# A two-layer graph network on one core: mended table rows for tied nodes, and edge slots that begin at any edge, fetched by SyncE at register addresses

## The chip, the core and the metric

The kernel runs on one core of one Trainium2 chip. The metric is the time on the device in microseconds (us), the median over several runs. The engines are TensorE (PE; its weight loads are PEld), VectorE (DVE), ScalarE (ACT), GpSimd (POOL) and SyncE (SP). They work in parallel, each through its own list of instructions in order, and wait for each other by semaphores. DMAs are issued from the lists of SP and POOL (a few from ACT) and move data beside them.

## The reference, cut to what matters

There are 3125 nodes of 256 features and 50000 edges sorted by their destination. Two layers follow each other:

```python
h = relu(layernorm(x))                              # layer 0
m = relu(h @ W_pool.T + b_pool)[src] * weight       # one row per edge
neigh = segment_max(m, dst); neigh = where(deg > 0, neigh, 0)
x = x + h @ W_self.T + b_self + neigh @ W_neigh.T + b_neigh

h = relu(layernorm(x))                              # layer 1
e = edge_emb[edge_type]                             # 16 types
messages = (h[src] + e) @ msg_W + msg_b
ew = 1 + edge_scale * tanh(gelu(concat(h[src], h[dst], e, task) @ att_W1 + att_b1) @ att_W2 + att_b2)
agg = segment_sum(scaled(messages) * ew, dst) / max(segment_sum(ew, dst), 1)
x = x + layernorm(h + mlp(concat(h, scaled(agg)))) * ln_g + ln_b
```

## The kernel before, in words

The nodes lie in 28 windows (NT) of 112 nodes (WIN), in 7 groups (NG) of 4 windows (GN). The program has five parts, called stages here.

**Stage 1** makes the rows that are gathered in layer 0 (`hp_d`, in HBM).

**The chain** (lines 424 to 1137) computes the segment maximum. Each of the 128 partitions owns a run of 391 edges (CH). In step j POOL gathers one row of 256 for each partition (line 683, a ring of 6 buffers of 4 steps, so POOL may be 24 steps ahead), ACT multiplies by the weight (716), and DVE keeps a running maximum that restarts where a new destination begins (924). SP stores the states in pieces of 8 steps (line 635, piece number q, 49 of them) to the table `hist_d`; the buffers of the states are a ring of 2, so step 8(q+2) waits until piece q has landed. The row of the table at a node's last edge is its maximum. Beside the chain DVE, PE and ACT do small jobs at step numbers written out by hand (`J_...`): the number of slots of each window, indices, products of weights. SP has loads between its stores, among them three at q = 24 and four at q = 28.

A node can span the border of two partitions. For these ties a scan over the partitions after the last step (1133) gives `carry`, the maximum that comes in from the partitions before. PE's step `choose(i)` (1365) places the carry rows for each window by a product with the one-hot `tied`, and DVE's `merge(i)` (1600) takes the maximum of them and the gathered rows.

**Edge slots.** The last-but-one stage works on slots of 128 edges that belong to one window. Before, a slot begins at a multiple of 32 edges (BLK): source, destination and type of the edges are written as blocks of 32 to `blocks_d`, the wanted blocks are gathered by POOL (1337, 14 gathers), written to `rec_d`, read back one group of 4 slots per partition (1295), and DVE turns them into rows (`slot_fields`, 1642); PE transposes them (`turn_fields`, 1425, 12 transposes) and DVE copies them out (`take_fields`, 1657). The number of slots is fixed at build time for the worst case: 425 slots in 107 groups, the last group with one slot.

**The node stage** (first half of the block from line 1226) loops over i = 0 to 6. POOL gathers the table rows of a group of windows (420, four gathers), `merge` mends them, PE transposes them (`turn_n`, 1376) and multiplies by W_neigh (`neigh`, 1385), DVE adds to x and takes the statistics (`rows_x`), POOL takes the inverse root (`root`, 1322), DVE makes the shifts (1623), ACT makes h (`rows_h`, 1521), PE transposes h (`turn_h`, 1396) and makes the tables of layer 1 (`messages`, 1408; `keys_q`, 1421 for i = 1 to 3, the other four at the end). PE's order is written out by hand: turn_n(i+1), turn_h(i), neigh(i+1), keys_q(i-1), three of four messages, choose(i+2), the last message. POOL's order is node_rows(i+2), root(i), record gathers. `keep_warm` are matmuls whose result nobody reads.

**The edge stage** does for each group of 4 slots: POOL gathers 128 rows of `pm_d` per slot (1354, a ring of 6 groups), PE makes z of each slot from the window's keys (1477, three products whose right side is at a register address) and the gathered rows (1479), ACT takes gelu (1565), DVE the dot product with W2 (1737), ACT the weights (1579 to 1586), PE sums by destination (1501) and DVE adds to `acc` at a register address (1724). The window numbers come to PE and DVE by a load of four registers per group (line 396). At every seventh group from group 6 on, 14 times, PE and ACT also do a pair of windows of another product (1490).

**The last stage** (from 1743) is the update of the nodes and the layernorm.

Of the kernel before, what the change touches and what calls it, by code (L numbers as in the profile page):

```python
# [6 lines left out]
def gnn_two_layers(nc, A, out):  # L7
# [15 lines left out]
    GN = 4  # L23
# [5 lines left out]
    BLK = 32  # L29
# [3 lines left out]
    NB = ER * ROW // BLK  # L33
    SG = 4
    RB = P // BLK
    SLOTS = (E + NT * (BLK - 1 + P - 1)) // P
# [3 lines left out]
    assert NGR <= P  # L40
    RC = -(-SLOTS * RB // P)
# [13 lines left out]
    hist_d = nc.dram_tensor("hist_d", [P * CH + 1, D], fp32, kind="Internal").ap()  # L55
    link_d = nc.dram_tensor("link_d", [P], fp32, kind="Internal").ap()
    blocks_d = nc.dram_tensor("blocks_d", [NB + 1, FLD * BLK], fp32, kind="Internal").ap()
    want_d = nc.dram_tensor("want_d", [RC * P], i32, kind="Internal").ap()
    rec_d = nc.dram_tensor("rec_d", [RC * P, FLD * BLK], fp32, kind="Internal").ap()
# [21 lines left out]
    with top:  # L81
# [38 lines left out]
        want = sbt("want", [P, RC], i32)  # L120
# [285 lines left out]
        keep = acc[0:WIN, after_nt + D:after_nt + D + NT]  # L406
# [9 lines left out]

        def node_rows(eng, i, to):
            for k in range(GN):
                t = i * GN + k
                eng.indirect_dma_start(to[:, k * D:(k + 1) * D], None, hist_d[:, :],  # L420
                                       bass.IndirectOffsetOnAxis(ap=end_i[:, t:t + 1], axis=0)).then_inc(ngot[i % 4], 16)

        b2 = ExitStack()
        with b2:
# [32 lines left out]
            end_0 = s("end_0", [WIN, NT], fp32)  # L457
            tied_b = s("tied_b", [P, WIN], fp32)
            tied_w = s("tied_w", [P, NT], fp32)
            tied = up[:, 2560:2560 + NT * WIN]  # L460
# [7 lines left out]
            blk = acc[0:ER, 8 * ROW:(8 + FLD) * ROW]  # L468
            junk = acc[:, 13 * ROW:14 * ROW]
            blk4 = blk.rearrange("p (b f e) -> p b f e", f=FLD, e=BLK)  # L470
            padb = s("padb", [1, FLD * BLK], fp32)
            cnt = s("cnt", [ER, NT + 1], fp32)
            j_i = s("j_i", [NGR, SG], i32)
            r_i = s("r_i", [NGR, SG * RB], i32)
            jf = s("jf", [NGR, SG], fp32)
            rf = s("rf", [NGR, SG * RB], fp32)
            s_f = s("s_f", [NGR, NT + 1], fp32)
            s_i = s("s_i", [NGR, NT + 1], i32)
            fb_i = s("fb_i", [NGR, NT + 1], i32)
            fb = s("fb", [NGR, NT + 1], fp32)  # L480
# [8 lines left out]
            wantf = s("wantf", [NGR, SG * RB], fp32)  # L489
            want_i = s("want_i", [NGR, SG * RB], i32)  # L490
            want_pad = s("want_pad", [1, RC * P - SLOTS * RB], i32)
# [9 lines left out]
            ngot = [sem2(f"ngot{r}") for r in range(4)]  # L501
            prep = sem2("prep")
# [27 lines left out]
            blk_ready = sem2("blk_ready")  # L530
            blk_out = sem2("blk_out")
# [1473 lines left out]
```

## Time and profile before

| What | Value |
|---|---|
| Time, median of 3 runs | 1336.85 us (1335.12 to 1338.69) |
| Profiled execution, its own time as the trace has it: the span | 1333.1 us |
| Mean granted TensorE clock | 0.80 of full speed |
| Busy shares | PE 71%, DVE 70%, POOL 65%, ACT 46% |
| DMA | 266.84 MB, mean 200 GB/s |
| Instructions | 18946 |

The trace is of one execution. Its span runs from the first to the last instruction; the timed runs lie some 2 to 6 us above it. In the rows further down, the number behind "idle" or in square brackets is the time that the engine had stood idle just before, with what ended it. In the timeline the columns are start, duration, engine, line, operation, tiles and count; consecutive instructions of one kind are merged into one row whose duration runs over all of them.

### The profile page before, as it was taken

The page shows a single profiled execution, that of the slowest core. Times are in us where ns is not written, and L with a number is a line of the kernel's source. Part 1 is how long each engine was busy: PE and PEld are TensorE (multiplying, and loading weights), DVE is VectorE, ACT ScalarE, POOL GpSimd, SP SyncE. Part 2 cuts the span into 40 slices and gives each one's busy share as a digit, 9 for nine tenths or more (in the row PEclk, how much of TensorE's full clock was granted, in tenths as well). Part 3 has the DMA queues.
Part 4 walks back from the last instruction along what each step waited for, and adds up shares of the span by engine and source line. Part 5 has one row for each costly group of instructions (what it writes and reads, how often), then busy time and mean ns, then how long its engine had stood idle before and what let it go on. Part 6 is the DMA issues. An engine that isn't in the chain of part 4 may idle for free. (4 is left out here: it accounts for less than half of the span.)

```text
span 1333.1 us, 18946 instructions
## 1 busy us (share of the span) xinstructions
PE 946.2 (71%) x5112; PEld 734.5 (55%) x5112; DVE 927.7 (70%) x2671; ACT 615.5 (46%) x1494; POOL 867.5 (65%) x884
## 2 busy tenths in 40 slices
PE   7405455555123511189997999999999999999984
PEld 6402233333012510177775777777777777777773
DVE  6466475666466554346756888888888888888758
ACT  6334333433333433323324666665656566666554
POOL 0377777777777777665237777777777777777112
PEclk9755555555555555599998999999999999999988
DMA  5667667557676665534657778778777877777322
GB/s 154 135 206 261 208 213 206 198 201 234 211 278 213 210 199 197 206 87 121 159 155 226 229 231 235 231 232 237 232 231 231 239 234 228 233 234 230 94 68 83
DMA packets 105353, 266.84 MB, mean 200 GB/s; under 512 B 25101, under 2 KB 45940, under 8 KB 99108
## 3 DMA queue, kind: packets, MB, share of 16 engines
q0 software_dynamic: 54560, 166.61, 42.7%
q1 hardware_dynamic: 48900, 97.26, 22.8%
q10 hardware_dynamic: 1792, 1.75, 0.5%
q8 instruction: 47, 0.77, 0.2%
q14 instruction: 54, 0.44, 0.1%
HBM read 195.59 MB, written 68.81 MB: 198 GB/s over the span
## 5 line engine op out<-in xcount | busy, mean ns | idle before, releaser
L683 POOL DMA_INDIRECT gath<-hp_d,chain_src x391 | 386.3, 988 | 169.3 <-issue 157.7
L1354 POOL DMA_INDIRECT gbuf<-pm_d,srcs x357 | 343.8, 963 | 114.7 <-issue 104.9
L924 DVE SCALAR_TENSOR_TENSOR hist<-hist,smask,gath 128x256 f32<-128x256 f32 x390 | 189.2, 485 | 207.4 <-ACT gath L716 199.6
L716 ACT ACTIVATE gath<-gath,chain_w 128x256 f32<-128x256 f32 x391 | 167.4, 496 | 335.3 <-DMA gath<-hp_d,chain_src 335.2
L1724 DVE TENSOR_TENSOR acc<-ps,acc 112x272 f32 x425 | 186.8, 440 | 70.2 <-DVE acc L1724 62.9
L1477 PE MATMUL ps<-qw,halves 128*128 x1275 | 209.9, 274 | 8.1 <-DVE halves L1709 8.1
L1479 PE MATMUL ps<-gbuf,ident 128*128 128x256 f32 x714 | 214.2, 382 | 0.0
L1565 ACT ACTIVATE gbuf<-ps 128x512 f32<-128x512 f32 x180 | 107.4, 597 | 163.8 <-PE ps L1479 163.8
L1501 PE MATMUL ps<-gbuf,placed 128*112 128x272 f32 x714 | 179.6, 393 | 0.9 <-issue 0.6
L839 PE MATMUL ps<-win_hot,node_hot 128*112 128x28 bf16 x391 | 43.6, 253 | 187.6 <-DVE win_hot L1023 187.6
L1477 PEld LDWEIGHTS ps<-qw,halves 128*128 128x128 bf16 x1275 | 125.0, 98 | 80.0 <-issue 11.2
L839 PEld LDWEIGHTS ps<-win_hot,node_hot 128*112 128x112 bf16 x391 | 39.9, 207 | 193.9 <-DVE win_hot L1023 192.6
L1501 PEld LDWEIGHTS ps<-gbuf,placed 128*112 128x112 f32 x714 | 125.6, 177 | 36.6 <-DVE acc L1724 2.8
L1737 DVE CUSTOM_DVE_ANT_0 gbuf<-gbuf,w2b 128x256 f32<-128x256 f32 x357 | 134.1, 427 | 10.2 <-ACT gbuf L1565 10.2
L1586 ACT ACTIVATE placed<-placed,logit 128x112 f32<-128x112 f32 x425 | 130.2, 377 | 3.5
L1479 PEld LDWEIGHTS ps<-gbuf,ident 128*128 128x128 f32 x714 | 108.5, 192 | 4.1
L765 PE MATMUL ps<-wsT,hT_s 128*112 128x256 f32 x112 | 57.2, 666 | 58.5 <-ACT hT_s L727 48.5
L1354 POOL DMA_INDIRECT attw<-pm_d,srcs x68 | 66.5, 978 | 21.6 <-issue 19.8
L765 PEld LDWEIGHTS ps<-wsT,hT_s 128*112 128x112 f32 x112 | 30.0, 298 | 79.8 <-issue 63.2
L1728 DVE TENSOR_TENSOR placed<-ps,edgef 128x448 f32<-128x448 f32 x107 | 65.8, 615 | 0.0
L1821 POOL TENSOR_TENSOR rs_c<-ve_c,power 112x4 f32<-112x4 f32 x7 | 12.5, 1788 | 75.2 <-DVE ve_c L1951 75.2
L1021 DVE TENSOR_TENSOR node_hot<-ps,low 128x896 bf16<-128x896 f32 (+1 forms) x49 | 52.9, 1081 | 0.0
(290 smaller groups left out, 1429.5 us busy)
## 6 DMA issues: line engine op xcount, KB each, us to landing
hist_d<-hist SPq DMA_DIRECT2D x48, 1024.0 KB, 4.5
gath<-hp_d,chain_src POOLq DMA_INDIRECT x391, 2.8
wn<-node_row_d SPq DMA_DIRECT2D x27, 224.0 KB
key<-node_row_d SPq DMA_DIRECT2D x26, 224.0 KB, 3.6
gbuf<-pm_d,srcs POOLq DMA_INDIRECT x357, 4.0
pm_d<-gbuf SPq DMA_DIRECT2D x6, 896.0 KB, 5.0
hb_d<-gbuf SPq DMA_DIRECT2D x7, 448.0 KB, 3.5
qw<-hb_d SPq DMA_DIRECT2D x7, 448.0 KB, 8.0
```

The source lines that it names most:

```text
L683: eng.indirect_dma_start(row_at(j), None, hp_d[:, :], bass.IndirectOffsetOnAxis(ap=chain_src[:, j:j + 1], axis=0)).then_inc(got[q % RINGG] ...
L716: eng.activation(row_at(j), row_at(j), ACT.Copy, scale=chain_w[:, j:j + 1]).then_inc(gw_ready, 1)
L765: ins = eng.matmul(bank(6, 2)[0:WIN, k * D:(k + 1) * D], hT[i % 2][:, (k * 2 + hf) * WIN:(k * 2 + hf + 1) * WIN], wsT[:, hf * D:(hf + 1) * ...
L924: eng.scalar_tensor_tensor(out=state_at(j), in0=state_at(j - 1) if j else first_state[:, :], scalar=smask[:, j:j + 1], in1=row_at(j), op0= ...
L1354: eng.indirect_dma_start(gath3(g % RING)[:, k, 0:2 * D], None, pm_d[:, :], bass.IndirectOffsetOnAxis(ap=srcs[:, g * SG + k:g * SG + k + 1] ...
L1477: eng.matmul(to, hot[g % 2][:, k * P:(k + 1) * P], qw[:, bass.ds(w[k] * (3 * D) + part * D, D)], start=part == 0, stop=False)
L1479: ins = eng.matmul(to, ident[:, :], gath3(r)[:, k, 0:D], start=False, stop=True)
L1501: eng.matmul(bank(4 + k)[0:WIN, 0:AW], place[q % 3][:, k * WIN:(k + 1) * WIN], gath3(q)[:, k, D:SW], start=True, stop=True).then_inc(sums_ ...
L1565: eng.activation(gath3(r)[:, 2 * half:2 * half + 2, 0:D], bank(2 * (g % 2) + half).rearrange("p (k d) -> p k d", k=2), ACT.Gelu)\
L1586: ins = eng.activation(at, at, ACT.Copy, scale=logit[q][:, k:k + 1])
L1724: eng.tensor_tensor(to, bank(4 + k)[0:WIN, 0:AW], to, ALU.add).then_inc(summed, 1)
L1737: ins = eng.tensor_tensor_reduce(zk, zk, w2b[:, :], 1.0, 0.0, ALU.mult, ALU.add, logit[r % 3][:, k:k + 1])
```

## The change

**Slots begin at any edge.** The blocks of 32 go. Source, destination and type are stored as three long rows (`fields_d`), and a slot is described by its first edge. The worst case falls to 418 slots in 105 groups, the last with two slots. In place of POOL's 14 block gathers, of `rec_d` and of its reading back, SP fetches each slot by a DMA of its own (3 runs of 512 bytes to one partition) whose address is in a register: 5 groups, that is 5 loads of four registers and 20 DMAs, after each of its stores from q = 24 to 44. `slot_fields` moves to chain step 376, `turn_fields` to PE's list ahead of the last matmuls of the chain, `take_fields` behind chain step 386; the row stores (`node_row_d`, `type_row_d`) move behind SP's last store of the chain.

**Tied nodes.** Only group 0 is still mended by `choose` and `merge`. For the other groups the 128 partitions' mended rows are computed once (one more POOL gather of the rows at the partitions' first ends, and one DVE maximum), stored by SP behind the table, and the row indices of tied nodes point there. POOL's gathers of group 1 now wait for that store.

```diff
-    SLOTS = (E + NT * (BLK - 1 + P - 1)) // P
+    SLOTS = (E + NT * (P - 1)) // P
...
-    hist_d = nc.dram_tensor("hist_d", [P * CH + 1, D], fp32, kind="Internal").ap()
+    hist_d = nc.dram_tensor("hist_d", [P * CH + 1 + P, D], fp32, kind="Internal").ap()
...
+            Q_SLOT, QG = 24, 5
+            J_ROWS = 376
+            J_COLS = J_ROWS + 4
...
+                def fetch_slots(n):
+                    if n == 0:
+                        eng.wait_ge(want_in, 32)
+                        eng.wait_ge(fld_out, 16)
+                    for g in range(n * QG, min(NGR, (n + 1) * QG)):
+                        regs = [eng.alloc_register(name=f"slot{g}_{k}") for k in range(SG)]
+                        eng.load(regs, starts[0:1, g * SG:(g + 1) * SG])
+                        for k in range(SG):
+                            e0 = eng.snap(regs[k], donate=True, min_val=0, max_val=E)
+                            eng.dma_start(flds3[g:g + 1, :, k * P:(k + 1) * P],
+                                          fields_d[:, bass.ds(e0, P)].rearrange("(a f) e -> a f e", a=1)).then_inc(slot_in[k], 16)
...
+                    if q >= Q_SLOT:
+                        fetch_slots(q - Q_SLOT)
+                eng.wait_ge(rows_ready, 2)
+                for d, t in ((node_row_d, row_n), (type_row_d, row_t)):
+                    for g0, g1 in ((0, EVEN), (EVEN, NGR)):
+                        eng.dma_start(d.rearrange("(g e) -> g e", g=NGR)[g0:g1, :], t[g0:g1, :]).then_inc(rows_out, 16)
...
                 node_rows(eng, 0, first_rows(0))
+                eng.indirect_dma_start(mend, None, hist_d[0:P * CH + 1, :],
+                                       bass.IndirectOffsetOnAxis(ap=first_end[:, 0:1], axis=0)).then_inc(mend_in, 16)
...
+                turn_fields()
                 eng.wait_ge(stepped, CH - 5)
                 for _ in range(14):
                     eng.matmul(bank(2)[:, 0:P], ident[:, :], ident[:, :], start=True, stop=True)
                 eng.wait_ge(stepped, CH)
+                eng.wait_ge(cols_taken, FLD)
...
+                    if j == J_ROWS:
+                        slot_fields()
+                    if j == J_COLS + 6:
+                        take_fields()
...
-                    t = at(j, J_LAST, 1, NT)
+                    t = at(j, J_LAST, 1, GN)
...
             def _(eng):
+                eng.wait_ge(mended, 1)
+                eng.dma_start(hist_d[P * CH + 1:P * CH + 1 + P, :], mend).then_inc(mend_out, 16)
                 eng.wait_ge(ngot[1], 16 * GN)
...
-                node_rows(eng, 1, first_rows(1))
                 eng.memset(power[:, :], -0.5).then_inc(power_set, 1)
                 eng.wait_ge(power_set, 1)
+                eng.wait_ge(mend_out, 16)
+                node_rows(eng, 1, first_rows(1))
...
                 def turn_n(i):
-                    eng.wait_ge(merged, i + 1)
-                    if i >= 1:
+                    if i == 0:
+                        eng.wait_ge(merged, 1)
+                    else:
+                        eng.wait_ge(ngot[i % 4], (i // 4 + 1) * (16 * GN))
                         eng.wait_ge(n_put, i)
...
-                choose(0)
+                choose()
                 keep_warm(12)
                 turn_n(0)
                 neigh(0)
-                choose(1)
-                keep_warm(8)
+                keep_warm(16)
                 for i in range(NG):
                     if i + 1 < NG:
                         turn_n(i + 1)
-                    if i == COL_AT:
-                        turn_fields()
                     turn_h(i)
                     if i + 1 < NG:
                         neigh(i + 1)
                     if 1 <= i <= QE:
                         keys_q(i - 1)
-                    messages(i, range(3))
-                    if i + 2 < NG:
-                        choose(i + 2)
-                    messages(i, range(3, GN))
+                    messages(i, range(GN))
...
+                def mend_rows():
+                    eng.wait_ge(mend_in, 16)
+                    eng.tensor_tensor(mend, mend, carry, ALU.max).then_inc(mended, 1)
...
-                merge(0)
+                merge()
+                mend_rows()
                 rows_x(0)
                 shifts(0)
-                merge(1)
```

Some small DVE jobs of the chain also change: 24 of 28 products for `tied` go, the slot arithmetic loses its block steps, and `tie` and `ends` get a few operations that count the first end of each partition and point tied nodes at their mended rows.

## Rows read from the trace of the kernel before

**Rows 1.** Busy time by stage, and of two short stretches, all engines
```profile
core 0: us, PE busy (x) PEld busy (x) DVE busy (x) ACT busy (x) POOL busy (x), PEclk, DMA share, GB/s
562.00:712.40 150.40, 132.70 (x690) 107.91 (x689) 89.47 (x169) 42.99 (x64) 71.65 (x65) 0.99 0.52 138
712.40:1250.00 537.60, 536.75 (x3064) 421.32 (x3064) 458.31 (x1576) 325.30 (x868) 395.78 (x412) 1.00 0.77 228
...
713.20:715.00 1.80, 1.75 (x7) 1.22 (x8) 1.17 (x3) 0.00 (x0) 1.45 (x2) 0.50 0.78 223
...
717.00:719.00 2.00, 2.00 (x15) 1.51 (x14) 0.88 (x5) 1.00 (x2) 1.70 (x2) 1.00 0.96 306
```
**Rows 2.** Line 683: ns min/median/max, first and last start
```profile
L683 POOL DMA_INDIRECT gath<-hp_d,chain_src x391: 942/946/2027, 52.4 to 556.7; - x196
```
**Rows 3.** Timeline, DVE in two groups of the edge stage, and its last sum
```profile
1228.25 0.61 DVE L1728 TENSOR_TENSOR placed<-ps,edgef 128x448 f32<-128x448 f32 x1
...
1233.23 0.62 DVE L1728 TENSOR_TENSOR placed<-ps,edgef 128x448 f32<-128x448 f32 x1
...
1259.18 0.44 DVE L1724 TENSOR_TENSOR acc<-ps,acc 112x272 f32 x1 [0.21 <-DVE acc L1724]
```
**Rows 4.** Timeline, POOL end of the chain, start of the mending
```profile
551.47 0.95 POOL L683 DMA_INDIRECT gath<-hp_d,chain_src  x1 [0.30 <-issue]
552.02 1.01 DVE L924 SCALAR_TENSOR_TENSOR hist<-hist,smask,gath 128x256 f32<-128x256 f32 x2
...
558.39 3.61 DVE L924 SCALAR_TENSOR_TENSOR hist<-hist,smask,gath 128x256 f32<-128x256 f32 x7 [5.36 <-ACT gath L716]
...
564.27 0.94 POOL L420 DMA_INDIRECT up<-hist_d,acc  x1 [6.68 <-DMA hist_d<-hist]
...
570.62 1.66 DVE L1600 SCALAR_TENSOR_TENSOR up<-ps,acc,up 112x256 f32<-112x256 f32 x4 [3.19 <-DMA up<-hist_d,acc]
...
581.45 1.05 POOL L1322 TENSOR_TENSOR acc<-acc,power 112x4 f32<-112x4 f32 x1 [2.62 <-DVE acc L1618]
...
585.15 0.93 PE L1396 MATMUL ps<-ident,gbuf 112*128 112x112 f32 x8
```
**Rows 5.** SP stores of line 635: ns min/median/max, and landings
```profile
L635 SPq DMA_DIRECT2D hist_d<-hist x51: 319/320/348, 74.9 to 562.0; - x51
...
DMA to landing us min/median/max: 2.0/4.4/8.3
```
**Rows 6.** take_fields and turn_fields, groups by line: busy, mean ns
```profile
L1662 DVE COPY edgef<-ps 128x428 f32<-128x428 f32 x2 | 1.1, 594 | 0.0
L1662 DVE CAST srcs<-ps 128x428 int32<-128x428 f32 x1 | 0.6, 594 | 0.0
...
L1431 PE MATMUL ps<-ident,qw 107*128 107x107 f32 x12 | 1.3, 255 | 0.0
```
**Rows 7.** Timeline, PE in the node stage
```profile
612.93 1.89 PE L1365 MATMUL ps<-acc,up 128*112 128x256 f32 x8
...
616.64 0.78 PEld L1376 LDWEIGHTS ps<-ident,gbuf 112*128 112x128 f32 x8 [0.51 <-DVE gbuf L1600]
...
634.52 0.78 PEld L1376 LDWEIGHTS ps<-ident,gbuf 112*128 112x128 f32 x8 [0.51 <-DVE gbuf L1600]
```
**Rows 8.** Timeline, PE at the start of the edge stage
```profile
713.25 0.82 PE L1477 MATMUL ps<-qw,halves 128*128 x3 [8.15 <-DVE halves L1709]
```
**Rows 9.** Register loads and address arithmetic of PE: ns min/median/max
```profile
L396 PEldq TENSOR_LOAD <-wins x107: 327/331/522, 712.0 to 1249.5; - x107
...
L1477 PEldq FUSED_REGOPS  x1275: 46/46/46, 713.1 to 1250.3; - x183
```
**Rows 10.** SP: small direct DMAs, and four loads at q = 28
```profile
L622 SPq DMA_DIRECT2D acc<-in_dst_dram x2: 268/272/275, 57.0 to 57.3; - x2
...
359.03 0.38 SPq L604 DMA_DIRECT2D acc<-in_L_gnn_ma_W_dram  x1
...
362.46 0.68 SPq L604 DMA_DIRECT2D acc<-in_L_gnn_ua_W_dram  x1
```

More of the change, by code:

```diff
@@ L39, in gnn_two_layers @@
     SLOTS = NGR * SG
-    assert NGR <= P
-    RC = -(-SLOTS * RB // P)
+    assert NGR <= P and E + P <= ER * ROW
     NPAD = 4000.0
@@ L536, in gnn_two_layers @@
             want_in = sem2("want_in")
-            recs_in = sem2("recs_in")
-            recs_out = sem2("recs_out")
-            nat_in = sem2("nat_in")
+            slot_in = [sem2(f"slot_in{r}") for r in range(4)]
+            shifted = sem2("shifted")
             rows_ready = sem2("rows_ready")
@@ L834, in type_messages, with turn_fields @@
                     ins.then_inc(tps, 1)
+                def turn_fields():
+                    eng.wait_ge(flds_ready, 1)
+                    for f, b in enumerate((6, 7, 4)):
+                        for k in range(SG):
+                            ins = eng.transpose(bank(b)[:, k * NGR:(k + 1) * NGR],
+                                                flds[:, f * GW + k * P:f * GW + (k + 1) * P], ident[0:NGR, 0:NGR])
+                        ins.then_inc(cols_ready, 1)
                 def count_ends(q):
@@ L1067, in tie @@
                     eng.tensor_scalar(tied_b[:, :], iof[:, 0:WIN], low[:, first], None, ALU.is_equal)
+                    eng.wait_ge(io_set2, 2)
+                    eng.tensor_copy(edge[:, 11:12], run_i[:, :])
+                    eng.tensor_scalar(off[:, :], own[:, :], own[:, first], 0.0, ALU.is_equal, ALU.add, accum_out=edge[:, 12:13])
                     after(eng.tensor_scalar(tied_w[:, :], iof[:, 0:NT], edge[:, 9:10], edge[:, 8:9], ALU.is_equal, ALU.mult))
+                    eng.tensor_scalar(tied_n[:, :], tied_w[:, :], edge[:, 11:12], None, ALU.mult)
+                    after(eng.scalar_tensor_tensor(out=edge[:, 13:14], in0=edge[:, 11:12], scalar=float(CH), in1=edge[:, 12:13],
+                                                   op0=ALU.mult, op1=ALU.add))
+                    eng.tensor_scalar(first_end[:, :], edge[:, 13:14], float(-(CH + 1)), None, ALU.add)
                 def ends(part):
@@ L1086, in ends @@
                                                        op0=ALU.add, op1=ALU.add))
+                        late = slice(GN, NT)
+                        after(eng.scalar_tensor_tensor(out=end_t[:, late], in0=bank(3)[0:WIN, late], scalar=float(P * CH),
+                                                       in1=end_f[:, late], op0=ALU.add, op1=ALU.subtract))
+                        after(eng.tensor_tensor(end_t[:, late], end_t[:, late], end_0[:, late], ALU.mult))
+                        after(eng.tensor_tensor(end_f[:, late], end_f[:, late], end_t[:, late], ALU.add))
                         eng.tensor_copy(end_i, end_f[:, :]).then_inc(ends_out, 1)
@@ L1178, in gnn_two_layers @@
             chosen = sem("chosen")
+            mended = sem("mended")
+            mend_out = sem("mend_out")
             merged = sem("merged")
@@ L1691, in _ @@
                         shifts(i + 1)
-                    if i + 2 < NG:
-                        merge(i + 2)
                     take(i, 3)
```

214 lines of the change are left out of this document (72 added, 142 removed).

## The prediction

> **What bounds the kernel now.** I read the busy time by stage first. The edge stage takes 537.6 us, and PE is busy for 536.8 of it at full clock; the node stage takes 150.4, with PE busy for 132.7, also at full clock [rows 1]. So both go at PE's pace, and there a PE instruction or a slot less is time. The chain is different: POOL issues 391 gathers from 52.4 to 556.7, one every 504.3 / 390 = 1.293 us [rows 2], and everything else in that stage only has to keep up, SP included. A piece of 8 steps lasts 10.34 us. The parts that the change moves into the chain are free if they fit beside that pace, and not otherwise.
>
> All sums are made against the profiled execution (span 1333.1). The median of the runs, 1336.85, lies 3.75 above it, and I carry that distance along.
>
> **Edge stage: fewer slots.** 425 slots in 107 groups become 418 in 105: 106 full groups and one slot before, 104 full groups and two slots after. A full group lasts 1233.23 - 1228.25 = 4.98 us [rows 3]. The 14 groups with the extra pair are longer, but they all stay. Two groups less: 2 x 4.98 = -9.96. The last group has one slot more, and the last sums follow each other at 0.44 + 0.21 = 0.65 [rows 3]: +0.65. **-9.3.** POOL would give about the same: a gather and its gap are 0.95 + 0.30 = 1.25 [rows 4], and seven of them 8.75.
>
> **Node stage: fewer products.** For i = 0 to 4 PE loses choose(i+2). Its eight matmuls show 1.89, of which the next ones overlap some 0.17 (an estimate): 1.72; and behind the last message PE stood 0.51 for DVE's merge before turn_n [rows 7]; both go: 5 x 2.23 = 11.15. The last step loses turn_fields ahead of turn_h(6), 1.3 [rows 6]. That makes 12.45. I take **-11.2**: with choose and merge gone, ACT's and DVE's lists come within about a microsecond of PE's in the three steps that hold keys_q, so some of it is kept back. The period to compare with is 634.52 - 616.64 = 17.88 [rows 7]; I expect 15.6 to 16.2. The 14 record gathers were POOL's, and PE did not wait for them; their removal counts nothing.
>
> **The start of the node stage gets longer.** Three costs.
>
> (a) take_fields runs behind chain step 386, in the middle of the last burst. DVE did the last seven steps in one go, 3.61 us, after standing idle 5.36 [rows 4]; the burst is steps 384 to 390. The copies, 0.6 + 1.1 = 1.7 [rows 6], come inside it and not in the idle time ahead. DVE's last step, SP's last store and POOL's first table gather all come **+1.65** later. The waiting PE transposes lose nothing by it, as they stand behind warm-up matmuls; the gathers are what merge waits for [rows 4].
>
> (b) Mending goes around by memory. Before: POOL's first table gather at 564.27, merge at 570.62, root(0) at 581.45, turn_h(0) at 585.15 [rows 4]. After, with (a) in: first gather 565.9, four more at 1.25 gives the mending gather at 570.9; as merge began some 2.6 behind the start of the fourth gather (564.27 + 3 x 1.23 = 568.0 to 570.62), it lands at 573.5. DVE's maximum of 128 x 256 about 0.5 (a chain step is 0.52): 574.4 with its queue. SP's store, a quarter of a piece of the chain, lands in 2.0 at best, 4.4 in the median of the large ones [rows 5]; I take 2.1, as it is small: 576.6. Now eight gathers, groups 1 and 2, stand ahead of root(0) on POOL: 8 x 1.25 = 10 less a gap, so root(0) starts at 586.4 instead of 581.45, and turn_h(0) follows at the same distance, about 590. That is **+4.9**, (a) included. PE then goes on at once into neigh(1), whose inputs are there early: -0.25.
>
> (c) PE stands idle for some 5 us between turn_n(1) and turn_h(0). After 8.15 us of idle time the granted clock was 0.50, that is 1.2 GHz, and four microseconds later 1.00, that is 2.4 GHz [rows 1, 8]. PE did 7 matmuls in 1.8 us against 15 in 2.0; at half speed for some three microseconds it loses about 1.5. From nothing (the clock stays) to 1.9; five is nearer eight than nothing, so **+1.5**. Together **+6.15**.
>
> **SP beside the chain.** This is the item that could turn the sign. After each store from q = 24 to 44 SP does 5 groups: a load of four registers, which costs PE 0.33 [rows 9], with gaps 0.45; and 20 DMAs. A direct DMA of one partition costs 0.27 [rows 10], 0.30 with its gap, and the address arithmetic 0.046 on PE [rows 9], 0.08 with its gap: 0.38 per slot. F = 5 x (0.45 + 4 x 0.38) = 9.85; with the store's 0.32 [rows 5] 10.2 per piece, against 10.34. It just fits. No row shows a DMA at a register address, so the price is bounded: below by the static 0.30 (F = 8.3), above by twice the arithmetic and a dearer DMA, 0.50 (F = 12.3). If SP falls behind, there is slack. A store lands in 4.4, so it may come 10.34 - 4.4 = 5.9 late. And POOL may run 24 steps ahead: at 551.47 it issues gather 386 or so while DVE does steps 382 and 383 [rows 4], and from step 368 on it would be free to go on, which leaves 15 steps, 19.4 us. The four loads at q = 28 take 4.1 [rows 10], the three at q = 24 at most as much; 5.9 + 19.4 - 8.2 = 17. So the loss is 21 x (F + 0.35 - 10.34) - 17: nothing up to 0.43 per slot. I count **0**.
>
> The Trainium skill has a rule against this change (DMA: Bandwidth & Descriptors, Latency and other measured facts): a register load has a floor of about 600 ns. PE's row shows 0.33 for the same load, and the row decides; by the page F would be 10.7 and the loss still about nothing.
>
> turn_fields (1.3 at full clock, twice that at half) ends on PE before the burst; slot_fields at step 376, about 1.5 us, lies under DVE's idle time. The row stores delay SP by some 4 us at the end of the chain, under POOL's table gathers. The small jobs of DVE net to less work, under the same cover.
>
> **Sum:** -9.3 - 11.2 + 6.15 = -14.35. Span 1318.7, time 1322.5.
>
> **The rivals.**
>
> *SP becomes the bound of the chain (slower), 0.22.* The mechanism is the loss above: with 0.50 per slot, 21 x 2.25 - 17 = +30, time 1352. The change loses as soon as the loss exceeds 14.35, at F = 11.5, or 0.46 per slot. For it: no reserve in my sum, and a kind of DMA that the trace does not hold. Against it: arithmetic and loads are cheap on two other engines, and SP's own list before is idle between stores.
>
> *The node stage does not follow, 0.10.* If the way over neigh, statistics, root, shifts and rows_h to turn_h binds as soon as PE's choose goes, the five steps keep their period: only turn_fields is saved. -9.3 + 6.15 - 1.2 = -4.35, time 1332.5. Against it: PE's idle time in a step is half a microsecond.
>
> *A cheaper start, 0.12.* The clock stays and the copies find room ahead of the burst: -1.5 - 1.65 more, time 1319.4.
>
> *A dearer start, 0.06.* Another 3 to 6 us by a slow store of the mended rows: 1326 to 1329. That the slots do not get fewer can be excluded: their number is fixed at build time.
>
> **How the numbers follow.** The forecast has 0.50, and its own range is 1319 to 1328. Measurement tells about 0.3%, 4 us, from no change. Faster (below 1332.8): forecast, cheaper and dearer start, half of the second rival, and the mild end of the SP case, together 0.74. Within 0.3%: 0.08. Slower: 0.18. For 8 in 10 the range goes from 1317 to 1345, which leaves out the bad half of the SP case and little below.
>
> **What would show it.** Right: the edge stage some 9.3 shorter at an unchanged 4.98 per group; PE's period in the node stage near 16; root(0) of the node stage about 23 behind the end of the last chain step instead of 19.5; POOL's gathers of the chain still at 1.293; SP's 20 DMAs and 5 loads of a piece within 10.8. Wrong: POOL or DVE in the chain waiting for the landing of a store after q = 24, and the chain's end moved from 562 to 580 or later; or turn_h starting behind PE's readiness in every step. If the slot DMAs cost 0.5, the forecast falls by its SP term alone, and the other terms can still be read from the later stages.

## The result: 16% slower, and where the time went

The kernel after takes 1554.40 us in the median (1553.27 to 1554.83), the kernel before 1336.41 beside it (four runs; 1336.85 is the median of three of them): a ratio of 1.163, 95% interval 1.161 to 1.165. The forecast was 1322.5, with a range to 1345. The profiled execution has a span of 1551.4, which is 218.3 more than before.

First the profile after, windows by stage: the chain from SP's first fetch to the last chain step, the node stage, the edge stage, and PE's turn_h(0).

```profile
core 0: us, PE busy (x) PEld busy (x) DVE busy (x) ACT busy (x) POOL busy (x), PEclk, DMA share, GB/s
322.00:796.40 474.40, 62.50 (x353) 53.87 (x354) 130.90 (x283) 83.98 (x206) 178.01 (x184) 0.50 0.34 113
796.40:939.90 143.50, 124.30 (x640) 102.60 (x639) 76.58 (x138) 42.53 (x64) 57.77 (x52) 0.95 0.48 133
939.90:1478.20 538.30, 536.40 (x3054) 420.32 (x3054) 457.59 (x1569) 324.45 (x866) 389.83 (x405) 0.99 0.76 224
822.50:824.20 1.70, 1.59 (x9) 1.59 (x10) 0.00 (x0) 0.86 (x2) 1.08 (x3) 0.50 0.31 95
```

The last chain step ends at 796.4, not 562.0 [rows 1]: +234.4. In that stretch no engine is busy for even 40% of the time, and the DMA queues carry 113 GB/s. From there to the first key match it is 143.4 us (150.4 before), the edge stage up to the last sum 538.3 (547.2 before, to 1259.62, the end of the last sum in [rows 3]), and the rest is 0.2 shorter. So +234.4 - 7.0 - 8.9 - 0.2 = +218.3. Two of the three stages did about what was forecast, and one item turned the sign.

The waits of the chain say what held it (line waited for: us in total, times, longest):

```profile
ACT gath L731 <- DMA gath<-hp_d,chain_src: 361.7, 51, 16.3
DVE hist L949 <- DMA hist_d<-hist: 332.3, 21, 17.9
POOL gath L696 <- DVE hist L949: 205.4, 26, 13.3
```

DVE's step (line 949) waits for the landing of a hist store, 21 times, 16 us each; hist has two buffers, so a piece of eight steps cannot start until the store of the piece before last has landed. POOL then waits for DVE, and ACT for POOL's gathers: those two are consequences. Before, this wait did not occur; line 924 waited for ACT. A store itself did not get slower (landing 3.9/4.2/8.3 us, min/median/max, against [rows 5]). It is issued late. SP's timeline shows behind what:

```profile
343.29 0.40 SPq L645 DMA_DIRECT2D hist_d<-hist  x1
344.40 21.20 SPq L639 DMA_DIRECT2D up<-fields_d  x20
365.65 0.41 SPq L645 DMA_DIRECT2D hist_d<-hist  x1
366.77 20.56 SPq L639 DMA_DIRECT2D up<-fields_d  x20
387.38 0.40 SPq L645 DMA_DIRECT2D hist_d<-hist  x1
```

Twenty fetches, with the five loads between them, take 21 us of SP, and the stores are 22 apart where they had been 10.34. By line (ns min/median/max, first and last start):

```profile
L636 SPq TENSOR_LOAD <-starts x105: 477/802/1142, 321.6 to 777.1; - x105
L639 SPq ALU_OP  x420: 32/36/55, 322.7 to 780.5; - x140
L639 SPq MOVE up<-fields_d x420: 29/29/42, 322.8 to 780.6; - x140
L639 SPq DMA_DIRECT2D up<-fields_d x420: 661/662/1137, 322.9 to 780.7; - x140
```

From start to start these are 0.83, 0.06, 0.07 and 0.71 us: 0.83 for a load and 0.84 for a slot. What remained open is why a fetch costs 0.66 us of SP, when the small DMA of [rows 10] cost 0.27: the address in a register, or the shape of the transfer.

### The profile page after: what moved, and what is told of

Same layout as the page of the kernel before. It is cut to its first block and busy times, and to the rows that moved or that the text cites. A ratio compares the mean times of both kernels' runs of the same rounds, so it can differ in the third digit from the quotient of the medians.

```text
span 1551.4 us, 19979 instructions
## 1 busy us (share of the span) xinstructions
PE 935.4 (60%) x5031; PEld 729.6 (47%) x5031; DVE 906.3 (58%) x2594; ACT 609.5 (39%) x1479; POOL 845.6 (55%) x864
## 5 line engine op out<-in xcount | busy, mean ns | idle before, releaser
L1374 POOL DMA_INDIRECT gbuf<-pm_d,srcs x350 | 338.5, 967 | 112.7 <-issue 103.4
L1702 DVE TENSOR_TENSOR acc<-ps,acc 112x272 f32 x418 | 183.6, 439 | 69.0 <-DVE acc L1702 62.1
L1482 PE MATMUL ps<-qw,halves 128*128 x1254 | 206.4, 274 | 8.1 <-DVE halves L1687 8.1
L1484 PE MATMUL ps<-gbuf,ident 128*128 128x256 f32 x700 | 210.5, 383 | 0.0
L1506 PE MATMUL ps<-gbuf,placed 128*112 128x272 f32 x700 | 175.4, 393 | 1.0 <-ACT placed L1589 0.8
L1715 DVE CUSTOM_DVE_ANT_0 gbuf<-gbuf,w2b 128x256 f32<-128x256 f32 x350 | 131.4, 426 | 10.7 <-ACT gbuf L1568 10.7
```

Of the source, the lines that this page charges most:

```text
L1374: eng.indirect_dma_start(gath3(g % RING)[:, k, 0:2 * D], None, pm_d[:, :], bass.IndirectOffsetOnAxis(ap=srcs[:, g * SG + k:g * SG + k + 1] ...
L1482: eng.matmul(to, hot[g % 2][:, k * P:(k + 1) * P], qw[:, bass.ds(w[k] * (3 * D) + part * D, D)], start=part == 0, stop=False)
L1484: ins = eng.matmul(to, ident[:, :], gath3(r)[:, k, 0:D], start=False, stop=True)
L1506: eng.matmul(bank(4 + k)[0:WIN, 0:AW], place[q % 3][:, k * WIN:(k + 1) * WIN], gath3(q)[:, k, D:SW], start=True, stop=True).then_inc(sums_ ...
L1702: eng.tensor_tensor(to, bank(4 + k)[0:WIN, 0:AW], to, ALU.add).then_inc(summed, 1)
L1715: ins = eng.tensor_tensor_reduce(zk, zk, w2b[:, :], 1.0, 0.0, ALU.mult, ALU.add, logit[r % 3][:, k:k + 1])
```

## The experiments

The record does not name the chip of the first comparison. The later runs were made in four sessions (the expectations say calls), on three chips (numbered 9, 12 and 1), and in each of them the kernel before took 1535 to 1542 us in the median, not 1336. Its trace there (b1_before) has 197 us more: 61 up to the end of the chain, 13 in the node stage, 123 in the edge stage. All engines are held up in some stretches (around 457 us PE stood idle for 2.62 us between single products and had nothing to wait for); why, and whether it has to do with the chip at all, is open. Each later run is read by its ratio to the kernel before of the same session, and by its own trace.

**1. The address or the shape.** e1_fixed writes constants in place of the registers:

```
-  regs = [...]; eng.load(regs, starts[0:1, g * SG:(g + 1) * SG])
-  e0 = eng.snap(regs[k], donate=True, min_val=0, max_val=E)
+  e0 = (g * SG + k) * 118
-  fields_d[:, bass.ds(e0, P)]
+  fields_d[:, e0:e0 + P]
```

> The changed kernel with the 420 slot fetches at addresses written into the program and no register loads; it leaves out the right slots' starts, so each slot holds other edges than it should, and the number of instructions after the fetch is the same. Theory A (SP issues too slowly, and the price is that of a DMA at a register's address, 0.66 us of instruction and 0.83 us from start to start, against 0.27 us for a small DMA at a fixed address in [rows 10]): SP's work for a piece of eight steps is 0.40 + 20 x 0.30 = 6.4 us, under the chain's 10.34, so no step waits; the last chain step ends near 562, not 796, and the time is 1554.4 - 234.4 = 1320, 1318 to 1323. Rival B (the shape costs it: three runs of 512 bytes onto one partition, whatever the address): 0.40 + 20 x 0.69 = 14.2 us for a piece, 21 x (14.2 + 0.35 - 10.34) - 17 = 71 us lost, 1390. Rival C (the DMA queues are full of small transfers and the hist stores land late, whoever issues them): as the changed kernel, over 1500.

It took 1598.20 against 1540.12, ratio 1.037 (1.031 to 1.043). A second run in another session:

> e1_fixed again, since the kernel before took 1540 us on the chip of the first call and 1337 on the chip of the first comparison, so that its ratio must be had beside a kernel before that is as in the profile; as there, it leaves out the right slots' starts. Rival B of that run, by what it showed (0.67 us from start to start): a piece of eight steps takes SP 0.40 + 20 x 0.67 = 13.9 us, loss 21 x (13.9 + 0.35 - 10.34) - 17 = 65 us on 1320: 1385, a ratio of 1.030 to 1.042. Theory A as it stood (the register's address is the whole price): 1320, a ratio of 0.987.

1599.36 against 1541.23, 1.038 (1.033 to 1.043). Theory A falls, and rival B's ratio holds in both: without any register a fetch of three runs takes 0.63 us. (Both forecasts count the store of a piece twice, as 0.40 and as 0.35, which makes them 7 us too high.)

e2_loads was to keep the register loads with constant addresses.

> As e1_fixed, but with the 105 register loads kept; it too leaves out the right slots' starts. The loads took about 0.80 us each in the changed kernel. Theory A: SP's work for a piece is 0.40 + 5 x 0.83 + 20 x 0.30 = 10.6 us, next to the chain's 10.34; by the formula of the prediction 21 x (10.6 + 0.35 - 10.34) - 17 is below zero, so the loss is nought to 5 us: 1320 to 1325, the same as e1_fixed within 5 us. If the loads are what holds SP (a wait for earlier DMAs in each), the time stays far above e1_fixed: over 1400. Rival B: 14.2 + 4.2 = 18.4 us for a piece, 160 us lost, 1480.

1.040 (1.034 to 1.046), but it tells nothing about loads: its trace holds no TENSOR_LOAD on SP at all, presumably because nothing used the registers. It is e1_fixed a third time. That is a lesson of its own: look in the trace whether the part that an experiment keeps is there.

e9_onerun lays the table out edge by edge, so that a fetch is one run of 1536 bytes, at a register's address as in the kernel after:

```
-  flds3[g:g + 1, :, k * P:(k + 1) * P]  <-  fields_d[:, bass.ds(e0, P)]          (3 x 512 B)
+  flds[g:g + 1, k * FLD * P:(k + 1) * FLD * P]  <-  fields_d[bass.ds(e0, P), :]  (1 x 1536 B)
```

> The changed kernel with the table laid out edge by edge (source, node and type of an edge side by side), so that each of the 420 fetches at a register's address brings one run of 1536 bytes in place of three of 512; the later steps read the same values at a stride. What e1_fixed showed first: without any register a fetch of three runs still took 0.627 us of SP, and 0.67 from start to start. Theory A2 (the three runs are the price; the register adds 0.17): a transfer of one run onto one partition took 0.293 us right behind another in the changed kernel (the load of the window numbers), so a fetch is 0.33 + 0.14 of arithmetic and gaps = 0.46 to 0.50 us, a piece of eight steps 0.40 + 5 x 0.80 + 20 x 0.46 to 0.50 = 13.6 to 14.4 us against 10.34; loss 21 x (13.6 to 14.4 - 10.34) - 9 to 17 = 52 to 76 us on 1320: 1372 to 1396, a ratio to the kernel before of 1.027 to 1.045. Rival A1 (the register's address is the price, whatever the runs): as the changed kernel, a ratio of 1.16.

1587.72 against 1541.23, 1.032 (1.027 to 1.037). Of the two theories A2 holds, but its ratio was met by luck: a slot took 0.41 us and not 0.46 to 0.50, and the loss was larger than the formula gives for that (section 3). The lines of both, first e1b_fixed, then e9_onerun:

```profile
L637 SPq DMA_DIRECT2D up<-fields_d x420: 3/627/1442, 362.1 to 699.6; - x140
```
```profile
L636 SPq TENSOR_LOAD <-starts x105: 1/554/1123, 367.6 to 686.6; - x105
L639 SPq FUSED_REGOPS  x420: 1/37/736, 369.0 to 688.5; - x140
L639 SPq DMA_DIRECT2D up<-fields_d x420: 2/228/1031, 371.8 to 688.7; - x140
```

The same bytes onto the same partition cost 0.63 to 0.66 us in three runs and 0.23 in one. The register adds 0.035 to the DMA (0.662 against 0.627) and about 0.13 of arithmetic and gaps; a slot by one run takes 0.41 from start to start. The load also became shorter, 0.55. A fetch of three runs also leaves two more packets of 4 bytes in the trace than a fetch of one; whether the runs are the price or this splitting, which came with them each time, these runs do not separate.

**2. Is it SP's queue?** b2_after runs the kernel after, unchanged, under the later conditions, and b1_before the kernel before, for its profile.

> The changed kernel, unchanged, beside the kernel before on this chip. By SP's rows, which are the same on both chips, a piece of eight steps takes SP 21.4 to 22 us here too, so 21 pieces take 450 to 462 us; e1_fixed took 14.5 for a piece and a ratio of 1.038 (59 us), e9_onerun 12.4 to 13 and more where SP was stalled, 1.032. Expected: e1_fixed's 1599 and 21 x (21.7 - 14.5) = 151 us more: 1750, a ratio of 1.136. If instead the loss on this chip is not SP's pace, a ratio under 1.08 or over 1.19.

1794.02 against 1534.57: 1.168 (1.163 to 1.174). The loss is about the same share as in the first comparison, but larger than was expected from e1_fixed. In the trace the pieces took 23.8 us in the median and not 21.7; in the stretches in which everything is held up, SP's instructions are held up too.

> The kernel before, unchanged, for its profile on the chip of the later calls, where it takes 1540 us and not 1337. Expected: the same durations of single instructions, a chain whose last step ends well after 562 us, and a chain's pace from store to store that varies; by that profile it can be read what pace a piece with 9.2 us of SP work (e4_one, ratio 1.02) had to keep. A time of 1530 to 1555.

1532.09. Its last chain step ends at 623.2, and its SP stores stand unevenly. Three rows of its Sync timeline:

```profile
476.92 0.32 SPq L635 DMA_DIRECT2D hist_d<-hist  x1
482.33 0.32 SPq L635 DMA_DIRECT2D hist_d<-hist  x1
512.10 0.32 SPq L635 DMA_DIRECT2D hist_d<-hist  x1
```

A piece takes 5.4 us, the next 29.8. Counted from step 192, the mean piece is 11.1 us, but the median is 6.6. In the first comparison it was 10.4 and 10.3. So DVE's steps are not bound to POOL's 10.34 in each piece: POOL is held up for shorter times, has gathers ready when DVE goes on, and DVE then catches up at 5.4 to 6.6. This matters for section 3.

e7_pool takes the fetches off SP and keeps everything else of the change. The table is e9_onerun's; the starts stay in SBUF, and POOL issues four gathers:

```
+  eng.indirect_dma_start(flds[:, k * FLD * P:(k + 1) * FLD * P], None, fields_d[:, :],
+                         bass.IndirectOffsetOnAxis(ap=want_i[:, k:k + 1], axis=0))   # k = 0 to 3
-  SP: 105 register loads and 420 fetches
```

> The whole change with the fetches on another queue: the same table edge by edge, and four gathers on POOL, one for each of the four slots of a group, that take their starts from a column of an SBUF tile and bring 128 edges each (384 values) onto 105 partitions, issued in the chain near step 230; SP issues none of the 420 fetches and no register is loaded. It computes everything. If SP's 420 issues were the whole loss: the chain ends as before, and the other parts stay as the changed kernel's trace has them (-7.0 from the last chain step to the first key match, -8.9 in the edge stage, -0.3 behind): 1554.4 - 234.4 = 1320.0, to which POOL's four gathers add at most 4 x 1.2 us in a stretch where POOL runs ahead of the chain: 1318 to 1325, a ratio of 0.986 to 0.992. Rival (the table's landing, the 420 slots' values or a busier queue delay the chain by themselves): over 1340.

1515.35 against 1541.23: 0.983 (0.979 to 0.987), a little better than was expected. Again, in a later session:

> e7_pool again. It computes everything. 0.979 to 0.990 of the kernel before.

1524.29 against 1541.68: 0.988 (0.984 to 0.992). The whole change with its 420 slots' fields fetched elsewhere is faster than the kernel before by 1.2 to 1.7%. Its four gathers (e7_pool), and what line 938, the chain step, waited for in e7b_pool (us in total, times):

```profile
L685 POOL DMA_INDIRECT up<-fields_d,want_i x4: 949/968/1013, 423.9 to 442.9; - x4
```
```profile
  ACT gath L720: 37.1, 8
  issue: 36.8, 13
...
  DMA hist_d<-hist: 1.0, 1
```

The wait for the stores (332 us in the kernel after, 392 in b2_after) is down to 1.0. An index gather brings 105 rows of 1536 bytes, each from any edge, for 1 us of POOL; SP needed 105 x 0.41 = 43 us for the same rows at best, and 88 in the kernel after.

**3. Threshold or share.** e3_three fetches three groups of five, e4_one brings a whole group by one fetch of three runs of 2048 bytes, e11_quarter does that without registers.

```
e3:  for g in range(n * QG, n * QG + 3)
e4:  flds3[g:g + 1, :, :] <- fields_d[:, bass.ds(e0, GW)]      (once for a group)
e11: flds3[g:g + 1, :, :] <- fields_d[:, e0:e0 + GW],  e0 = g * 472
```

> The changed kernel with three of five groups fetched for each piece (63 groups of 105; the other slots hold edges that one plain transfer puts there, and so the wrong ones). Theory A, a threshold: a group takes (21.92 - 0.75) / 5 = 4.2 us of SP, a piece with three 12.8 to 13.5 us against the chain's 10.34, so the loss is 21 x (12.8 + 0.35 - 10.34) - 17 = 42 to 21 x (13.5 - 10.34) - 9 = 57 us: 1362 to 1377. If instead each fetch costs the chain its share, with no threshold (a port or the queues): 0.6 x 234 = 141 us, 1461.

> The changed kernel with one fetch for a group, at one register's address, of three runs of 2048 bytes instead of four fetches of three runs of 512: the bytes are the same, the instructions a quarter; it leaves out the right starts of three of four slots. Theory A: SP's work for a piece is 0.40 + 5 x (0.80 + 0.83) = 8.6 us, under 10.34, no loss: 1318 to 1323, as e1_fixed. If bytes or the transfers themselves hold the stores back: 1500 and over. If the loads do: as e2_loads, whatever that is.

> e4_one again beside e11_quarter; it leaves out the right starts of three of four slots. If this call falls on the chip with the 1541 us: a ratio of 1.01 to 1.03, since 9.2 us are over the pace of the pieces between stalls, and 25 to 50 us behind e11_quarter. If it falls on a chip where the kernel before takes 1337: within 4 us of e11_quarter, since 9.2 is under 10.37.

> e4_one without registers: one fetch for a group at an address written into the program, three runs of 2048 bytes, 105 in all; it leaves out the right slots' starts. SP's work for a piece of eight steps is 0.4 + 5 x 0.67 = 3.8 us in place of 9.2, the transfers are the same. Theory: what counts is SP's piece against the pace that the chain can reach between its stalls (5.4 to 6.6 us on this chip, median 6.6; 10.2 on the first); 3.8 is under both, so no loss is left: a ratio of 0.982 to 0.990, as e7_pool's. Rival (105 transfers of 6 KB cost by themselves, or their values' late landing does): as e4_one, 1.01 to 1.03.

The table has SP's work for a piece without hold-ups (the sum of the median distances from start to start), then what a piece took SP in the trace (from the start of a store to the end of the last fetch behind it) and the distance between stores, both as means of the 21 pieces from q = 24 to 44, the ratio, and the end of the last chain step. The kernels without fetches on SP, e7_pool and e7b_pool, ended their chain at 638.3 and 633.8; in single traces of one kernel this end differs by up to 14 us.

```
kernel        work    took    store to store   ratio (95%)             chain ends
after         21.3    22.0    22.1             1.163 (1.161 to 1.165)  796.4 (first comparison)
b2_after      21.3    24.9    25.0             1.168 (1.163 to 1.174)  906.7
e1b_fixed     13.9    16.2    16.3             1.038 (1.033 to 1.043)  714.8
e9_onerun     11.6    15.4    15.5             1.032 (1.027 to 1.037)  704.3
e3_three      13.0    16.4    16.5             1.047 (1.041 to 1.054)  724.1
e4b_one        8.8    14.4    14.5             1.024 (1.018 to 1.030)  702.3
e11_quarter    3.8     5.5    12.0             0.993 (0.988 to 0.998)  645.5
e7b_pool       0.4            11.0             0.988 (0.984 to 0.992)  633.8
```

e3_three took 1610.59 against 1540.12. The four executions of e4_one lie between 1546 and 1584, too far apart for a ratio; e4b_one repeats it. The loss does not go by the number of fetches: with 252 of 420, e3_three's chain ended 88 us behind e7_pool's mean of 636, and the kernel after 271 behind; a share of 0.6 would be 163. It stands 9 us behind e1b_fixed, though by the sum of medians it has less work on SP; what its pieces took SP in the trace was as much, 16.4 against 16.2. The loss does not go by bytes or transfers either: e4b_one and e11_quarter have the same 105 transfers of the same form, and 8.8 against 3.8 us of SP work make 45 us (1575.06 against 1529.91 in one session). What line 949 of e4b_one, the chain step, waited for:

```profile
  DMA hist_d<-hist: 162.2, 20
  issue: 42.1, 20
  DVE hist L949: 23.6, 31
  ACT gath L731: 16.5, 2
```

In e11_quarter no wait for a store is among the first four (2.7 us in all).

The columns "took" and "store to store" say it most directly. In every kernel that lost, SP was occupied from one store to the next: behind its last fetch it had 1 to 3 us left in all 21 pieces together, and 137 in e11_quarter. The stores came when SP came to them. In e4b_one 8.8 us of work, which are under the mean pace of 11.1, took 14.4, because SP's instructions were held up as well. They are also over the 5.4 to 6.6 at which DVE catches up. Each of the two could turn 8.8 us into a loss, and these runs do not separate them. (e11_quarter itself has 0.993 where 0.982 to 0.990 was forecast; its interval reaches into that range, and e7b_pool beside it has 0.988.) The formula of the prediction knows neither: for the work of e9_onerun it gives 21 x (11.6 - 10.34) - 17 = 9 us and for e1b_fixed 58, and they stand 72 and 84 above e7_pool in the same session. Whether 9 us cost nothing where the pieces are even, as in the first comparison, was not tried.

**4. The mended rows alone.** e5_mend is the kernel before with the mended rows and nothing of the slots.

```
+  POOL: node_rows(0), then one gather of the first end of each partition's run into mend
+  DVE:  tensor_tensor(mend, mend, carry, max);   SP: store mend behind hist_d's rows
+  POOL: node_rows(1) waits for that store
-  PE: choose(1) to choose(6);   -  DVE: merge(1) to merge(6)
```

> The kernel before with the mended rows alone, its slots at multiples of 32 edges as they were (nothing of the slots, the fetches or the edge stage is changed). By the traces: the node steps' period falls from 17.88 to about 15.9 us with six of them, less -0.25 at the end, against +3.0 us from the first gather to the first turn and the slower clock's 1.5; turn_fields and take_fields stay in the last node step. Expected: -11.2 + 4.5 = -6.7 us, and 1330, 1328 to 1333, a ratio of 0.993 to 0.997. Rival (the gain of the node stage comes from the 14 record gathers that left POOL, not from the mended rows): 1336 to 1341, the same as before or slower.

1531.86 against 1541.23: 0.993 (0.990 to 0.996). The size is as forecast, and the rival falls: the rows gain something with the record gathers in place. The steps of the node stage are the distances of PE's turn_h. On e5_mend's timeline they start so, from turn_h(1) on (turn_h(4) is the last row):

```profile
678.28 0.99 PE L1427 MATMUL ps<-ident,gbuf 112*128 112x112 f32 x8 [0.81 <-ACT gbuf L1548]
...
699.17 1.76 PE L1427 MATMUL ps<-ident,gbuf 112*128 112x112 f32 x8 [4.78 <-ACT gbuf L1548]
...
718.12 0.93 PE L1427 MATMUL ps<-ident,gbuf 112*128 112x112 f32 x8
...
734.07 0.93 PE L1427 MATMUL ps<-ident,gbuf 112*128 112x112 f32 x8
```

The step 718.12 to 734.07 is the 15.95 that was expected, but 678.28 to 699.17 is 20.9, longer than before, with PE idle for 4.78. The record gathers are the obvious suspect. POOL's timeline, and behind it DVE's:

```profile
681.20 1.15 POOL L1366 DMA_INDIRECT qw<-blocks_d,want  x1 [0.30 <-issue]
...
686.35 0.93 POOL L422 DMA_INDIRECT gbuf<-hist_d,acc  x1 [0.30 <-issue]
687.31 1.05 POOL L1350 TENSOR_TENSOR acc<-acc,power 112x4 f32<-112x4 f32 x1
```

```profile
696.16 0.69 DVE L1661 COPY gbuf<-ps 112x512 f32<-112x512 f32 x1 [4.86 <-remote]
696.77 0.15 DVE L1654 SCALAR_TENSOR_TENSOR acc<-acc 112x4 f32<-112x4 f32 x1
```

root(2) does stand directly behind nine gathers in a row, five of them record gathers. But PE did not wait for it: root(2) had ended at 688.4, and the shifts that need it (1654) began at 696.77, behind a copy of DVE (1661) whose input PE had finished at 690.2 and which began 6.0 us later. e6_mend_first, described below, settles it. It has the same nine gathers directly ahead of root(2), and its step from turn_h(1) to turn_h(2) is 15.8 us:

```profile
671.05 0.93 PE L1427 MATMUL ps<-ident,gbuf 112*128 112x112 f32 x8
...
679.08 0.93 POOL L422 DMA_INDIRECT gbuf<-hist_d,acc  x1 [0.30 <-issue]
680.03 1.05 POOL L1350 TENSOR_TENSOR acc<-acc,power 112x4 f32<-112x4 f32 x1
...
686.89 0.93 PE L1427 MATMUL ps<-ident,gbuf 112*128 112x112 f32 x8
```

So the 20.9 is one of the hold-ups, and the prediction's zero for the record gathers stands. In the next step, 19.0 long, the products with W_neigh took 5.75 us instead of 3.71, at a granted clock of 0.53 behind that idle time. (In e6_mend_first that step has 17.4; why it is not 15.9 is open.) Where e5_mend's 0.7% sits cannot be read from one profile here: beside b1_before its chain ends 8 us later, its node stage is 2 us shorter, and the edge stage, in which nothing was changed, 4. In e6_mend_first's trace the node stage is 8.1 us shorter than in b1_before's.

e6_mend_first and e8_best issue the mending gather ahead of the first rows, on top of e5_mend and of e7_pool.

> e5_mend in the same other order: the mending gather ahead of the first rows on POOL and the mending ahead of the merge on DVE, with the slots as before. Expected: 1 to 4 us under e5_mend, a ratio of 0.990 to 0.993 where e5_mend had 0.993. Rival: no change from e5_mend.

> e7_pool with two things in another order: POOL issues the mending gather ahead of the four gathers of the first rows, and DVE mends ahead of the merge. It computes everything. The second gather of rows waits for the mended rows' round trip through memory (4.9 us on POOL before node_rows(1)'s rows), so the round trip then begins about 4 x 1.2 us earlier, while the first rows come 1.2 us later. Expected: 1 to 4 us faster than e7_pool: a ratio to the kernel before of 0.979 to 0.983 where e7_pool had 0.983. Rival (the later first rows move the first turn by as much as the second is helped): within 1 us of e7_pool.

> e8_best again, in the same call as e7_pool: it computes everything. The traces of the two (first gather to first turn, and the second rows) say at most 2 us either way: within 5 us of e7b_pool. If the other order helps as first thought, 1 to 4 us under it.

e6_mend_first took 1527.57 against 1534.57, 0.994 (0.991 to 0.997), and e5_mend 0.993. e8_best took 1520.49, 0.990 (0.986 to 0.993); beside each other, e8b_best has 0.988 (0.984 to 0.992) and e7b_pool 0.988. No gain; both forecasts of 1 to 4 us fall. In e8b_best's trace node step 0 is 6.4 us shorter than in e7b_pool's (12.0 against 18.4), and turn_h(0) starts 5.5 us later behind the chain; ACT began its first copy of the stage 5.4 us after PE had finished its input. The same copy is 8.1 us late in e8_best and 8.2 in e6_mend_first, so in all three traces of this order; of the others only b1_before has it (7.9). Whether the order causes this delay, and whether it would help without it, stays open.

## Why the prediction was wrong, point by point

**SP beside the chain: the step that failed.** The prediction set 0.38 us for a slot and 0.45 for a load, F = 9.85 per piece, and counted 0. Measured: 0.84 for a slot and 0.83 for a load, so F = 5 x (0.83 + 4 x 0.84) = 21. The upper bound of 0.50 was no bound. It took its DMA price from one row of another shape [rows 10] and let a guess at the arithmetic stand for all that was unknown, when the DMA itself went from 0.27 to 0.66. Most of that comes with the three runs (0.63 with a constant address, 0.23 for one run at a register's), which no row of before shows for one partition. But the same rows had a warning: two of the four weight loads stand there at 0.38 and 0.68 us of SP, and the four together took 4.1, so a direct DMA had no one price on SP. And the load was priced on PE [rows 9], where it took 0.33; on SP it took 0.80. The Trainium skill's rule (DMA: Bandwidth & Descriptors, Latency and other measured facts: a floor of about 600 ns for a register load) was nearer to SP than PE's row was: 0.80 in the kernel after, 0.55 in e9_onerun. As a floor it does not hold here, since the 0.55 and PE's 0.33 lie under it. A row of one engine had been given the last word on another. The prediction's own estimate by that figure is also off: with 0.60 in place of 0.33 and the same gap F is 9.85 + 5 x 0.27 = 11.2, not 10.7, and the loss by its formula 8 us, not nothing.

**The form of the loss was right for the first comparison.** 21 x (21 + 0.35 - 10.34) - 17 = 214, against 234.4 measured. Of the rest, 12 us are that a piece took 21.9 and not 21.35; the other 8 would fit a reserve smaller than 17, which was not measured. In the later sessions it came out too low (section 3): it compares the price of SP's work without hold-ups with the mean pace of a chain whose pieces are even, and there neither is so.

**The chance.** "SP becomes the bound" was named as the rival, with the wait that then came, at 0.22, but priced at 1352, and so the range ended at 1345. An item with no row of its own, repeated 420 times in the queue that stores the chain's results, deserved a range in which each 0.1 us of a slot is 21 x 20 x 0.1 = 42 us.

**Edge stage, -9.3: right.** It became 8.9 shorter. A group lasts as long as it did: 1455.80 - 1450.81 = 4.99 us against 4.98 [rows 3], from DVE's timeline:

```profile
1450.81 0.61 DVE L1706 TENSOR_TENSOR placed<-ps,edgef 128x448 f32<-128x448 f32 x1
...
1455.80 0.61 DVE L1706 TENSOR_TENSOR placed<-ps,edgef 128x448 f32<-128x448 f32 x1
```

**Node steps, -11.2, period 15.6 to 16.2: right.** On PE's timeline neigh comes every 15.9 us, against 17.88 [rows 7], and from turn_h(0) to turn_h(6) it is 85.4 us instead of 95.3: 9.9 less, although the slower clock's 1.5 (below) is in it.

```profile
837.29 3.71 PE L1407 MATMUL ps<-wn,acc 128*112 128x256 f32 x16 [0.24 <-ACT acc L1516]
...
853.18 3.71 PE L1407 MATMUL ps<-wn,acc 128*112 128x256 f32 x16 [0.29 <-ACT acc L1516]
```

That the record gathers count for nothing was right as far as the traces show: e6_mend_first keeps them and has a step of 15.8.

**The start of the node stage, +6.15: right within a microsecond.** The way of the mended rows is read from the timeline of all engines: the mending gather, DVE's maximum, SP's store, the second group's first gather, root(0), turn_h(0).

```profile
792.88 0.59 DVE L1042 CAST srcs<-ps 128x420 int32<-128x420 f32 x1
793.39 1.09 DVE L1042 COPY edgef<-ps 128x420 f32<-128x420 f32 x2
794.39 2.04 DVE L949 SCALAR_TENSOR_TENSOR hist<-hist,smask,gath 128x256 f32<-128x256 f32 x4
...
798.75 0.94 POOL L416 DMA_INDIRECT up<-hist_d,acc  x1 [45.47 <-DMA hist_d<-hist]
...
803.68 0.95 POOL L708 DMA_INDIRECT up<-hist_d,first_end  x1 [0.30 <-issue]
...
806.73 0.42 DVE L1608 TENSOR_TENSOR up<-up,acc 128x256 f32<-128x256 f32 x1
807.17 0.35 SPq L1311 DMA_DIRECT2D hist_d<-up  x1
...
809.63 0.94 POOL L416 DMA_INDIRECT up<-hist_d,acc  x1 [4.88 <-DMA hist_d<-up]
...
819.19 1.06 POOL L1348 TENSOR_TENSOR acc<-acc,power 112x4 f32<-112x4 f32 x1
...
822.61 1.76 PE L1418 MATMUL ps<-ident,gbuf 112*128 112x112 f32 x8 [5.05 <-ACT gbuf L1526]
```

From the first table gather to turn_h(0) it is 23.86 against 20.88 [rows 4]: +3.0, forecast 4.9 - 1.65 = 3.25. PE was idle for 5.05, the granted clock then was 0.50 (last row of the windows above), and turn_h(0) took 1.76 instead of 0.93 [rows 4]; with the start of neigh(1) that is about the 1.5 us that were forecast. take_fields stands inside the last burst, as forecast, four steps before its end. Its 1.65 us and the 7.0 together: -11.2 + 6.15 - 1.65 = -6.7 from the last chain step on, measured -7.0.

So -6.7 and -9.3 stand at -7.0 and -8.9. With SP's term at nothing the sum would have been met: the first comparison's other terms add up to -16.1 against -14.35, and in the later sessions the kernel without SP's fetches has 0.983 and 0.988, beside the forecast's 1322.5 / 1336.85 = 0.989.

## What to carry to other kernels

Price a DMA on the engine that issues it, with its own number of runs, and multiply by its count before you call it hidden; where no row shows that form, the item needs a range of its own, not a zero. Measure in the trace how long a helper queue is occupied in each round of the main chain, and how much time it has left: the sum of its single durations was 8.8 us where it was occupied for 14.4, and staying just under the mean pace was not enough. Many small fetches from computed places can be one gather with a column of indices, if the table is laid out so that a fetch is one run.

## What was not expected of the hardware

- A fetch of 1536 bytes onto one partition took SP 0.63 us in three runs of 512 bytes at a constant address, 0.66 at a register's, and 0.23 in one run at a register's. Three runs of 2048 bytes took 0.64 to 0.70: it is not the bytes.
- A load of four registers took 0.80 us on SP behind such fetches and 0.55 behind the one-run ones; PE's took 0.33 [rows 9].
- POOL's gather moved 105 rows of 1536 bytes from a table whose rows are 12 bytes long, starting at any row, in 0.97 us of issue.
- The same kernel took 1336 us in one session and 1527 to 1555 in four others on three chips, with the same durations of single instructions (DVE's chain step 0.485 us, POOL's gather 0.946) and pauses between them.
